# Head norm with its factors from PSUM and x1's rounding one batch later, in an mLSTM cross-attention with an MX FFN

## The reference, cut to what is computed

```python
# x, ctx: (8, 256, 512); 16 heads of 32; Wi, Wf: (1536, 16); w_gate, w_up: (2048, 512); w_down: (512, 2048)
q = layernorm(x); k = v = ctx
ig, fg = [q, k, v] @ Wi + bi, [q, k, v] @ Wf + bf
log_D = tril(cum(log_sigmoid(fg))_s - cum(...)_t) + ig_t        # per head, 256 x 256
D = exp(log_D - max_t log_D)
C = (q_h @ k_h.T / sqrt(32)) * D
h = (C / (max(|C.sum|, exp(-max)) + 1e-6)) @ v_h
hn = (h - mean(h)) * rsqrt(var(h) + 1e-6) * ln_scale            # over the 32 of a head
x1 = x + hn
def q_mx(z, mantissa): ...    # blocks of 32: power of two of the block's maximum, round, clamp
y = layernorm(x1)
inter = silu(q_mx(y) @ q_mx(w_gate).T) * (q_mx(y) @ q_mx(w_up).T)
out = x1 + q_mx(inter) @ q_mx(w_down).T
```

## Time and profile before

| | |
|---|---|
| runs | 544.37, 546.87, 1383.94 us (median 546.87) |
| profiled execution | 548.92 us, span 547.0 us, mean TensorE clock 0.877 |
| busy | PE 449.5 us (82%), DVE 434.3 (79%), POOL 249.9 (46%), ACT 243.2 (44%) |
| chain that ended last | PE 42%, issue 18%, POOL 17%, DVE 13%, ACT 4%, DMA 3% |
| batch loop, 150 to 340 us | PE 151.5, DVE 161.7, POOL 97.4, ACT 92.3 busy, clock 0.79 |
| FFN, 340 to 547 us | PE 187.7, DVE 161.9, POOL 95.9, ACT 77.4 busy, clock 0.97 |

### The profile page before, as it was taken

The page is one execution under the profiler, slowest core; times in us unless marked ns, Lnnn a source line. Parts: engine busy times, 40 slices in busy tenths (PEclk is TensorE's granted clock), DMA queues, the critical chain, the costliest instruction groups (busy, mean ns, idle before and its releaser), DMA issues.

```text
span 547.0 us, 10343 instructions
## 1 busy us (share of the span) xinstructions
PE 449.5 (82%) x3465; PEld 299.6 (55%) x3465; DVE 434.3 (79%) x615; ACT 243.2 (44%) x341; POOL 249.9 (46%) x228
## 2 busy tenths in 40 slices
PE   0697988399778686959789698799799999999993
PEld 0597988168556465657658384344344444444441
DVE  5569886679798897979789876798978888888781
ACT  1656663246354363726264464244344434434431
POOL 2444541232553537264644564755334353354443
PEclk9997885579978797987859577799989999999999
DMA  7455621143231413141420203011111111111211
GB/s 225 155 185 168 224 98 38 42 120 116 84 114 59 140 59 120 24 146 48 131 67 20 77 2 116 1 38 40 38 40 40 68 47 38 38 38 39 76 38 38
DMA packets 30566, 43.73 MB, mean 80 GB/s; under 512 B 6980, under 2 KB 11972, under 8 KB 30532
## 3 DMA queue, kind: packets, MB, share of 16 engines
q1 hardware_dynamic: 27280, 42.80, 23.8%
q10 hardware_dynamic: 3252, 0.46, 0.5%
HBM read 34.41 MB, written 8.85 MB: 79 GB/s over the span
## 4 chain that ended last, share of the span: by engine, by line
PE 42%; issue 18%; POOL 17%; DVE 13%; ACT 4%; DMA 3%; POOLq 1%; SPq 0%; DVEq 0%; ACTq 0%
PE psA L1359 8%; PE psA L1368 8%; PE psC L1386 7%; PE psC L1193 4%; POOL early L615 3%; PE psB L1378 3%; PE psA L1256 2%; PE psC L1236 2%; DMA early<-in_x_dram 2%; POOL wq L552 2%; POOL kTa L678 2%; POOL xc L648 2%; PE psA L1165 2%; DVE qTa L1128 2%; DVE pam L941 2%
## 5 line engine op out<-in xcount | busy, mean ns | idle before, releaser
L678 POOL TENSOR_TENSOR kTa<-kTa,ps 128x1024 bf16<-128x1024 bf16 x32 | 62.0, 1937 | 100.8 <-DVE kTa L1131 100.8
L1284 PE MATMUL psA<-vp,DC 128*128 128x128 f32 x512 | 72.4, 309 | 12.1 <-DVE DC L1035 12.1
L1284 PEld LDWEIGHTS psA<-vp,DC 128*128 128x128 f32 x512 | 70.1, 223 | 14.1 <-issue 14.1
L552 POOL TENSOR_TENSOR wq<-wq,ws 128x1024 bf16<-128x1024 bf16 x24 | 50.6, 2108 | 51.9 <-DVE wq L969 51.9
L1359 PE MATMUL psA<-WgT,qTa 128*128 128x512 bf16 x256 | 64.7, 399 | 2.5 <-ACT hf L823 2.5
L1368 PE MATMUL psA<-WuT,qTa 128*128 128x512 bf16 x256 | 63.1, 391 | 1.2 <-DVE kTa L1119 1.2
L1386 PE MATMUL psC<-WdT,kTa 128*128 128x512 bf16 x256 | 60.5, 379 | 2.4 <-ACT kTa L888 2.4
L888 ACT ACTIVATE kTa<-psB 128x1024 bf16<-128x1024 bf16 x32 | 32.8, 1024 | 58.1 <-PE psB L1378 57.9
L1119 DVE TENSOR_TENSOR kTa<-kTa,psA 128x1024 f32<-128x1024 f32 x32 | 39.0, 1219 | 19.4 <-PE psA L1368 19.4
L1035 DVE SCALAR_TENSOR_TENSOR DC<-psA,DC 128x512 f32<-128x512 f32 x64 | 41.0, 684 | 13.5 <-ACT DC L814 10.7
L814 ACT ACTIVATE DC<-psB 128x512 f32<-128x512 f32 x64 | 37.2, 597 | 20.1 <-PE psB L1270 19.6
(11 more groups left out here) (132 smaller groups left out, 857.8 us busy)
## 6 DMA issues: line engine op xcount, KB each, us to landing
early<-in_x_dram SPq DMA_DIRECT2D x16, 512.0 KB, 4.0
wraw<-in_L_ffn_w_down_dram SPq DMA_DIRECT2D x8, 512.0 KB, 5.6
early<-in_ctx_dram SPq DMA_DIRECT2D x8, 512.0 KB, 4.8
wraw<-in_L_ffn_w_gate_dram SPq DMA_DIRECT2D x8, 512.0 KB, 4.3
wraw<-in_L_ffn_w_up_dram SPq DMA_DIRECT2D x8, 512.0 KB, 3.4
x_scratch<-early SPq DMA_DIRECT2D x8, 512.0 KB, 3.0
kTa<-x_scratch SPq DMA_DIRECT2D x16, 256.0 KB, 2.7
out_dram<-kTa SPq DMA_DIRECT2D x16, 256.0 KB, 2.0
```

What stands on the lines that cost most here:

```text
L552: nc.gpsimd.tensor_tensor(blocks(wq[p][:, :]), blocks(wq[p][:, :]), spread(ws4[p][:, :], UB), ALU.mult).then_inc(wq_ready.sem, 1)
L678: nc.gpsimd.tensor_tensor(blocks(pd[h]), blocks(pc[h]), spread(ps4[h][:, :], PB), ALU.mult).then_inc(pq_ready.sem, 1)
L1284: last = nc.tensor.matmul(psA[:, j, to:to + P], DC[n % DCN][:, i4 * P:(i4 + 1) * P], values[:, left:left + P], start=i4 == 0, stop=c == 0, ...
```

## The change

1. The layer scale and the roots are multiplied by PE. A table `ltab` (32 x 512) holds ln_scale on the block diagonal of heads (made once by two affine selects on POOL). Each batch PE transposes the 32 roots of a row into psC[1] (`root_transpose`), ACT copies them to `rT` (`copy_root`), and two fp32 products rT x ltab put root times scale for every column into psC[1] and psC[0] (`scale_root`). `head_norm` reads its factor from there, one chunk of 512 columns at a time, and POOL's multiplication by `lns` goes.
2. `x1_round`, `x1_norm` and `back_x` of a batch stand one step later; so two batches (6 and 7) are rounded in the FFN's first tiles, in three pieces (`x1_amax`, `x1_scale`, `x1_clamp`).
3. `head_norm` and `x1_stats` stand behind the second four decay products, the head power on ACT behind the copy of the state, and the weight evacuations and transposes are moved.
4. Small tables share memory (pam, pinv, ps4 with weight tables, xinv with xam), and DVE and POOL have the first two and last two steps written out.

```diff
--- before.py
+++ after.py
...
-        lns = sb("lns", [P, E])
+        ltab = sb("ltab", [DROW, E])
+        rT = sb("rT", [DROW, NCH * P])
...
+                own = ltab[:, :].rearrange("r (h d) -> r h d", d=DH)
+                nc.gpsimd.affine_select(out=own, in_=own, compare_op=ALU.is_ge, fill=0.0, base=0,
+                                        pattern=[[-1, NH], [0, DH]], channel_multiplier=1).then_inc(ltab_step, 1)
+                gp.wait_ge(ltab_step, 1)
+                nc.gpsimd.affine_select(out=own, in_=own, compare_op=ALU.is_ge, fill=0.0, base=0,
+                                        pattern=[[1, NH], [0, DH]], channel_multiplier=-1).then_inc(ltab_step, 1)
+                gp.wait_ge(ltab_step, 2)
...
-            def last_power(b):
+            def last_power(b, c):
                 gp.wait_ge(hv_ready.sem, hv_ready.at(b, 1))
-                nc.gpsimd.tensor_tensor(sm[:, 0].rearrange("p c h -> p (c h)"), sm[:, 3].rearrange("p c h -> p (c h)"),
-                                        mhalf[:, 0:1].broadcast_to([P, NCH * NH]), ALU.pow).then_inc(hr_ready.sem, 1)
+                last = nc.gpsimd.tensor_tensor(sm[:, 0, c, :], sm[:, 3, c, :], mhalf[:, 0:1].broadcast_to([P, NH]), ALU.pow)
+                if c == NCH - 1:
+                    last.then_inc(hr_ready.sem, 1)
...
-                gp.wait_ge(hn_ready.sem, hn_ready.at(b, 1))
-                ch.link(nc.gpsimd.tensor_tensor(hn, hn, lns[:, :].unsqueeze(1).broadcast_to([P, NCH, E]), ALU.mult))
+                gp.wait_ge(hn_ready.sem, hn_ready.at(b, 2))
...
@@ gpsimd, step
+                second = isinstance(b, int) and b == 1
                 if not first:
                     head_rsqrt(b - 1)
+                w_back(2 * b + B + 1, 1)
+                if not (first or second):
+                    back_x(b - 2)
+                if not last:
+                    carry_q(b + 1, 1 - p)
                 if not first:
                     residual(b - 1)
                 if not last:
-                    carry_q(b + 1, 1 - p)
-                w_back(2 * b + B + 1, 1)
+                    w_back(2 * b + B + 2, 0)
                 if not first:
                     x1_rsqrt(b - 1)
                 if not last:
-                    w_back(2 * b + B + 2, 0)
                     weigh(b + 1, 1 - p)
-                if not first:
-                    back_x(b - 1)
...
@@ gpsimd, behind the batches
-            last_power(B - 1)
             back_p(0, 0)
+            last_power(B - 1, 0)
             back_p(0, 1)
-            residual(B - 1)
+            last_power(B - 1, 1)
             back_p(1, 0)
             back_p(1, 1)
+            residual(B - 1)
             add_x1(0, 0, 0)
-            x1_rsqrt(B - 1)
             back_p(2, 0)
             back_p(2, 1)
             add_x1(1, 1, 0)
             back_p(3, 0)
-            back_x(B - 1)
+            back_x(B - 2)
             back_p(3, 1)
             add_x1(2, 0, 1)
-            with gp.Fori(0, TILES // 2 - 2) as i:
+            x1_rsqrt(B - 1)
+            for t in range(4, 8):
+                back_p(t, 0)
+                if t == 6:
+                    back_x(B - 1)
+                back_p(t, 1)
+                add_x1(t - 1, (t - 1) % 2, (t - 1) // 2)
...
+            def copy_root(b):
+                act.wait_ge(r_mm.sem, r_mm.at(b, 0))
+                act.wait_ge(rt_mm.sem, rt_mm.at(b, 1))
+                nc.scalar.activation(rT[:, :], psC[1][0:DROW, 0:NCH * P], ACT.Copy).then_inc(rt_ev.sem, 1)
...
@@ scalar, step
-                evac_gate_up(2 * b + B, 0, b)
-                if not first:
-                    head_power(b - 1)
+                second = isinstance(b, int) and b == 1
+                if not (first or second):
+                    x1_norm(b - 2)
                 copy_h(b, p, 0)
                 exps(b, 4)
                 exps(b, 5)
+                evac_gate_up(2 * b + B, 0, b)
                 copy_v(b, p, 1)
-                if not first and not (isinstance(b, int) and b == 1):
-                    evac_xq(b - 2)
                 copy_state(b, p)
+                if not first:
+                    head_power(b - 1)
                 exps(b, 6)
                 exps(b, 7)
+                if not first:
+                    copy_root(b - 1)
                 if not last:
                     round_const(2 * b + B + 2, 0)
-                if not first:
-                    x1_norm(b - 1)
                 copy_h(b, p, 1)
-                evac_gate_up(2 * b + B + 1, 1, b)
...
+                if not (first or second):
+                    evac_xq(b - 2)
+                evac_gate_up(2 * b + B + 1, 1, b)
...
-            def head_norm(b, p):
-                ve.wait_ge(hr_ready.sem, hr_ready.at(b, 1))
-                nc.vector.tensor_tensor(sq.rearrange("p c h d -> p (c h) d"),
-                                        hf[p][:, :, :, 0:DH].rearrange("p c h d -> p (c h) d"),
-                                        spread(sm[:, 0].rearrange("p c h -> p (c h)"), NCH * NH),
+            def head_norm(b, p, c, bank):
+                ve.wait_ge(r_mm.sem, r_mm.at(b, c + 1))
+                nc.vector.tensor_tensor(sq[:, c], hf[p][:, c, :, 0:DH],
+                                        psC[bank][:, :].rearrange("p (h d) -> p h d", d=DH),
                                         ALU.mult).then_inc(hn_ready.sem, 1)
...
+            def x1_round(b):
+                x1_amax(b, ch)
+                x1_scale(b, ch)
+                x1_clamp(b)
...
@@ vector, step
             def step(b, p, n, first, last):
                 for k in range(HPC):
                     c_mult(b, k)
+                if not last:
+                    w_front(2 * b + B + 2, 0, b + B // 2 + 1)
                 if not first:
                     head_var(b - 1, 1 - p)
-                if not last:
-                    w_front(2 * b + B + 2, 0, b + B // 2 + 1)
                 w_round(2 * b + B + 1, 1)
-                if not first:
-                    head_norm(b - 1, 1 - p)
+                if not (first or isinstance(b, int) and b == 1):
+                    x1_round(b - 2)
                 for k in range(HPC, 2 * HPC):
                     c_mult(b, k)
                 if not last:
                     w_pow(2 * b + B + 2, 0)
                 if not first:
-                    x1_stats(b - 1)
+                    head_norm(b - 1, 1 - p, 0, 1)
+                    head_norm(b - 1, 1 - p, 1, 0)
                 if not last:
                     w_front(2 * b + B + 3, 1, b + B // 2 + 1)
                     w_round(2 * b + B + 2, 0)
                 if not first:
-                    x1_round(b - 1)
+                    x1_stats(b - 1)
                 if not last:
                     w_pow(2 * b + B + 3, 1)
-            pipeline(ch, ve, step)
-            head_var(B - 1, 1)
+            pipeline2(ch, ve, step)
...
@@ vector, behind the batches
             pair(0, 0)
+            head_var(B - 1, 1)
             pair(0, 1)
-            head_norm(B - 1, 1)
             pair(1, 0)
+            head_norm(B - 1, 1, 0, 1)
             pair(1, 1)
+            head_norm(B - 1, 1, 1, 1)
+            pair(2, 0)
+            x1_amax(B - 2, fch)
+            pair(2, 1)
+            x1_scale(B - 2, fch)
+            pair(3, 0)
+            x1_clamp(B - 2)
+            pair(3, 1)
             x1_stats(B - 1)
-            pair(2, 0)
-            pair(2, 1)
-            pair(3, 0)
-            x1_round(B - 1)
-            pair(3, 1)
-            with ve.Fori(0, TILES // 2 - 2) as i:
+            pair(4, 0)
+            pair(4, 1)
+            pair(5, 0)
+            x1_amax(B - 1, fch)
+            pair(5, 1)
+            x1_scale(B - 1, fch)
+            pair(6, 0)
+            x1_clamp(B - 1)
+            pair(6, 1)
+            pair(7, 0)
+            pair(7, 1)
...
+            def root_transpose(b):
+                root = sm[:, :, :, :].rearrange("p k c h -> p (k c h)")
+                pe.wait_ge(hr_ready.sem, hr_ready.at(b, 1))
+                for c in range(NCH):
+                    last = nc.tensor.transpose(psC[1][0:DROW, c * P:(c + 1) * P], root[:, c * NH:c * NH + DROW], ident[:, :])
+                last.then_inc(rt_mm.sem, 1)
+            def scale_root(b, c, bank):
+                pe.wait_ge(rt_ev.sem, rt_ev.at(b, 1))
+                nc.tensor.matmul(psC[bank][:, :], rT[:, c * P:(c + 1) * P], ltab[:, :], start=True, stop=True).then_inc(r_mm.sem, 1)
...
@@ tensor, step
             def step(b, p, n, first, last):
-                w_transpose(2 * b + B, 0, rows_order)
                 for k in range(HPC):
                     heads(b, p, k)
                 decay(b, p, 4)
                 decay(b, p, 5)
+                w_transpose(2 * b + B, 0, rows_order)
                 centre(b, 1)
                 qk(b, 1)
-                if b >= 2:
-                    pe.wait_ge(wT_ev.sem, wT_ev.unit(2 * b + B))
-                    x_transpose(b - 2)
                 state(b)
                 decay(b, p, 6)
```

(33 more changed lines are left out.)

82 lines of the change are left out of this document (48 added, 34 removed).

## The result

The changed kernel takes 562.0 us (median of 4 runs, 560.6 to 562.9); the kernel before took 545.7 beside it. The ratio is 1.031 [1.026, 1.035]: slower, and outside the range of 529 to 560. Medians here are of all executions of a kernel, the ratios leave out executions over 1.5% above its fastest. The profiled execution took 561.9 with a span of 560.4, against 547.0 before, so 13.4 us are to be found; the medians lie 16.3 apart, since the profiled execution of the kernel before (548.9) was 3.3 above its median.

The account below looks back on a forecast made before the run. No engine alone was taken to set the time; DVE and PE chains were read stage by stage. Batches 2 to 6 -3.1, batch 1 -4.6, batch 7 +2.1 and FFN +3.5 gave -2.1: 545 us, range 529 to 560.

Parts of the forecast that it names:

- DVE's waits: In the batch loop, DVE's 2.25 us wait for POOL's residual goes, as does ACT's 5.98 before x1's norm.
- The 29.1: DVE's time per loop batch: 25.8 plus 0.1 of work plus 3.2 of collisions with POOL, range 28.2 to 30.1 us.
- (a): Loop collision: POOL's weight step behind the second rounding outlasts the statistics and holds DVE's next TENSOR_SCALAR 0.4 us.
- (b): Loop collision: POOL's other weight step falls on late x1's power, inverse and scale: 0 to 1.9 us, taken as 0.9.
- (c): Loop collision: x1's last step and carry_q on POOL outlast the four products beside them, costing 0.7 us on w_pow.
- (d): Loop collision: POOL's residual runs beside a reduction, then holds the power and inverse: 1.2 us.
- PE's ring: PE's loop chain: 26.7 us of work plus steps off PE, about 30.3 per batch, 27 if the clock stays up.
- Between 29.1 and 30.3 I take 29.8: Time for each of batches 2 to 6, against 30.4 before: -3.1 us in five.
- Batch 7 to the gate: From batch 7's first product to the first gate product: 24.2 us against 22.1 before, +2.1.
- FFN, +3.5: First FFN tiles: 10.3 us of root work, power wait, DVE pieces and collisions against an excess of 6.8, so +3.5.
- The root product's price, 1.16: Each fp32 root product of 512 columns on PE takes 1.16 us: 2.3 for both, 4.1 as upper end.
- PE's root chain decides: Rival: root products cost 2.04 us each on the lowered clock, loop ring 32.1, total 561; chance 0.17.

Follow-up runs that it names:

- e12: e10 with POOL's four large loop operations cut to 32 columns per part, that work left out: 528.7 us, ratio 0.970.
- e8: Changed kernel with batch 7's roots taken like other batches', ahead of the FFN, and x1's transpose (behind all head products) and evacuation moved forward: 545.1 us, ratio 1.002.
- e7: Changed kernel with four bf16 products that compute nothing put on PE where it waits for the roots, each batch 1 to 7: 551.6 us, ratio 1.011.
- e11: e10 with the filling products of e7 in PE's wait for the roots, in the loop alone: 539.4 us, ratio 0.988.
- e10: e8 with batch 7's root work on PE moved behind the up products and both head norms behind half tile (0,1): 543.7 us, ratio 0.994.
- e13: Changed kernel with the same four filling products as e7, placed behind the next batch's decay product 3, ahead of x1's transpose: 555.0 us, ratio 1.012.
- e3: Changed kernel with the roots' part undone: DVE reads roots from SBUF, POOL multiplies by layer scale, no root work on PE: 562.9 us, ratio 1.030.

## Why the prediction was wrong

Three steps failed. The sum for batch 7 left the root work on PE out and had the head products at the upper clock: 24.2 us to the first gate product, 32.3 measured. The FFN's wait for the power, put at about 1, made +3.5 of what was +8.3. And the loop's batch was taken between two bounds, 29.8, where it is 30.5.

- **DVE's waits: right; its row 1.4 too short.** The waits of 2.25 and 5.98 went. The 29.1 was made of 24.5 of own work, 1.35 of small idle gaps (30.38 - 26.40 - 2.25 - 0.38) and 3.2 of collisions. The own work is 24.5 (e12's busy time). Collisions are 28.3 - 24.5 = 3.8, inside the 2.3 to 4.2. (a) is 0.4 as placed and (b) came in one batch of five, 0.3 on average for 0.9; but w_pow (L996, 1.9 us) lost 1.3 for the 0.7 of (c), in three batches to the weight step and not to x1's, and (d), on L979, was 1.9 for 1.2. The idle gaps are 2.2, of which DVE waits 0.9 for ACT's exponentials and PE's root products.
- **PE's ring: right as a size.** PE's work was put at 26.7 and is 26.6, the ring at 30.3, and the batch is 30.5.
- **"Between 29.1 and 30.3 I take 29.8": wrong.** Where two engines' rows depend on each other, the batch takes the longer one or more, not a value between. DVE's row too came to 30.5: 24.5 + 3.8 + 2.2. 30.5 instead of 29.8 is 3.5 us in five batches, of the 15.5 between the forecast of -2.1 and the 13.4 of the traces.
- **Batch 1: right**, 25.0 against 25.2. It has neither x1's rounding nor the second wait.
- **Batch 7 to the gate, 24.2 against 32.3: the largest miss.** The sum had 14.2 to DVE's last product; it is 17.1 (324.74), since PE waits 2.0 for x1's evacuation, begins the head products 0 to 3 4.8 us behind DVE's first product, takes 5.42 for them at the lowered clock, and the QK products stand behind them. With the evacuation forward (e8) it is 13.3. It then had head products and inter at 5.2; between 324.74 and their end at 335.28 lie 10.5: the root products stand ahead of the head products (the edit's cost that was counted for the loop was left out of this sum), and these take 6.5 at the lowered clock instead of 3.8. The chain behind it, 4.8 in the sum, was 4.7. e7 takes 6.6 off and e8 7.1, of a miss of 8.1; the two don't add up, e11 has both and takes 25.4. What e8 keeps is the root products and a lowered clock on the head products (6.4).
- **FFN, +3.5 against +8.3.** Root work on PE (2.8) was right: 0.61 and twice 1.12. "About 1" for the power was not: cutting it in two made 2.90 + 3.00 of 5.42, PE waits 2.26 for it, the gate products behind lose 1.3 to the clock, and DVE waits 4.80. The moved roundings were not the trouble: e10 has all of them and ends in 213.7.
- **The root product's price, 1.16: right**, the pair took 2.5 in the changed kernel. e7 shows 1.98 for two on the upper clock and e13 3.75 on the lower, so 0.99 and 1.88 each. The four passes that the Trainium skill states (FP8 and Floating Point Precision, TensorE Precision Notes) gave an estimate of 0.85, near the upper one; the trace is 0.14 above it. By itself, without a second one behind it, a product takes 1.12. The rule would have moved the sum by 0.6 us per batch; the clock of the products behind moved batch 7 by 2.7.
- **The rival "PE's root chain decides", 561**, gave the time, but not by its own terms: it had batches of 32.1 (30.5), +3.5 for batch 7 (+10.3) and +5.5 for the FFN (+8.3). It had the root products on the lowered clock and left out the head products behind them, which lost more. That these ran on the lower clock behind that wait is what e7 shows. That its time came near 562.0 was luck: each of its terms was off, and the errors cancelled.
- **Tells.** A gate product 24 us behind batch 7's start was named as the sign, and it was the one that failed. The two signs of being wrong did not show it: batches were not 27, and PE's waits before the transposes were 1.0 in most batches, 2.3 at most, and never over 4. A sign on the clock behind that wait was missing.

## What to carry to other kernels

When one engine is relieved by giving work to another, write both rows out as chains with their waits and take the longer; an average of two bounds is no bound. Ask for each new wait of PE what stands behind it, and price that at the lower clock; and sum the last, unhidden batch and the first tiles behind the loop piece by piece, because there the moved work is on the path in full. If relief of either engine alone gives 1 us, try both at once before calling either of them harmless: here that gave 3.8.

## What the runs showed of the hardware

Behind waits of 1.0 + 0.5 us of PE the same 16 fp32 products took 6.5 us (granted clock 0.56) instead of 3.8 (1.00), and with bf16 products that compute nothing in that wait the kernel took 551.6 us instead of 562.0 (e7). That the wait alone lowers the clock is not shown: it still stands at 1.00 during the root transposes behind the first wait (262.90 to 263.80 in the changed kernel) and falls during the root products. Whether it falls differs between batches of the same program (5.5, 3.8 and 6.6 in batches 3, 4 and 5 of e7).

The power function on POOL costs by elements, and cutting it in two saves nothing: 128x16 took 2.90 and 3.00, 128x32 5.42; two operations on ACT (Ln and Exp) and four short ones on POOL give the same roots in 1.9 us (325.43 to 327.31 in e8).

DVE's head norm with one input in PSUM kept 0.67 us in the middle of a POOL operation of 2.36. The Trainium skill (SBUF — State Buffer, Who interferes with whom) says that such an operation does not contend, and the trace agrees. In e3 the norm with both inputs in SBUF took 2.28 beside POOL. That run, which also gives POOL its 2.4 us back, has batches 1.3 us longer; it can't tell the two apart.
